# Wo as two groups of seven block products in the second to fourth pair of chunks

## The chip, the cores and the metric

One core of a Trainium2 chip runs the whole program in one launch. The metric is the device time of that launch in microseconds (us); smaller is better. Five engines take part: PE (matrix products), DVE (VectorE), ACT (ScalarE), POOL (GpSimd) and SP, which only issues transfers. Each works through its own list of instructions in order and is held by semaphore waits written into that list.

## The reference

`x` is (8, 512, 512) in float32: 8 chunks of 512 tokens by 512 features.

```python
xn = layernorm(x)
q, k, v = xn @ Wq.T + bq, xn @ Wk.T + bk, xn @ Wv.T + bv
kv = cumsum((elu(k) + 1) * v, axis=tokens)              # no matrix: a running sum per feature
s = ((elu(q) + 1) * kv * SCALE) @ Wo.T + bo             # "context" @ Wo
h = silu(fwht(xn * SU_ug) @ W_gate.T * ..) * (fwht(xn * SU_ug) @ W_up.T * ..)   # 2048 wide
g = silu(fwht(h * SU_dp) @ W_down.T * ..)
out = x + s * g
```

Wq, Wk, Wv and Wo are 512 by 512, gate and up 512 to 2048, down 2048 to 512. `fwht` is folded into the weights once.

## The kernel before

**Precision and products.** Every float32 operand is held as two float16 parts, HI and LO, and each product of blocks takes three matmuls per 128 rows of contraction: HI by HI, HI by LO, LO by HI. Each matmul is 128 by 128 by 512.

**Pairs, groups and seven products.** The 8 chunks go in four pairs. In pair 0 the weights are prepared, and products are plain (`plain_tile`). In pairs 1 to 3 a *group* `g` treats two 128-row blocks of a weight (rows `fp` and `fp + 2`) against the two chunks of the pair and both halves of the contraction, as a 2 by 2 product of blocks by the Strassen-Winograd scheme: seven products P1 to P7 of 6 matmuls each (`product`, L1639) in place of eight. That takes sums of weight blocks (S1 to S4, made in `s_sums` L1216, `s_high` L760, `s_low` L1232) and of token blocks (T1 to T4, `x_sums` L1074, `t_low` L1090, `t_high` L705). There are 22 groups (`GROUPS`): 6 for K, V, Q, then gate and up in turn, gate at even `g`, up at odd `g`, `g` from 6 to 21.

**A group on PE** (`group`, L1655) is P4 of `g-1`, P6, P3 of `g-1`, P2, P7, P1 of `g+1`, P5. P1, P6, P7 and P4 go into one "chain" bank, copied out between them by ACT (`copy_sum`, L798, line L803); P2 and P5/P3 go into two other banks, and DVE adds them (`add`, L1102, line L1107). The four result tiles of a group are called C11, C22, C21, C12, in this order of work; C21 is read from the chain bank itself. P1 of `g+1` uses the chain bank of `g-1` and waits until C21 of `g-1` has been taken from it (`wait_bank`, L1616). P7 of `g` waits for ACT's copy of P6 (`copied`).

**A group on DVE** (`group`, L1440), in order: for `g-1` use C22, `hidden_low` C11, use C21, `hidden_low` C22, add C12; add C11 of `g`; for `g-1` use C12, `hidden_low` C21; add C22 of `g`, which waits for P5 of `g`, the group's last product; `hidden_low` C12 of `g-1`; use C11 of `g`. Then, in pair 1 alone, `s_low` of one late weight piece and `s_sums` of the next; then, in pairs 1 and 2, statistics of the next pair at `g` 16 and 18. "Use" of an up tile is `hidden` (L1146), of a gate tile nothing: so for even `g` DVE handles the up tiles of `g-1` in it.

**A group on ACT** (`group`, L874): copies after P6, P7 and P1, between them silu of gate tiles (L826) or the float16 part of up tiles (`hidden_high`, L833), and in pair 1 `s_high` (L770) after the copy of P1 of `g+1`.

**Late weight pieces.** The sums S1 to S4 of pieces 0 to 11 are made in pair 0; pieces 12 to 21 are made in groups 5 to 14 of pair 1 (`late_sums`). POOL loads each raw piece (512 KB, `load_blocks`, L627, issue L641) as soon as `s_sums` of the one before is done, and stores the sums (L646).

**Down and Wo.** Behind the groups PE runs, per chunk, four quarters of down (`down_part`, L1736: 192 matmuls per chunk) and then Wo as a plain product (`out_product`, L1766: 4 tiles of 12 matmuls, L1788). Before them DVE takes the context's maximum (`ctx_absmax` L1170), a scale from it (`ctx_scale`, L1177), and splits its eight tiles in HI and LO (`split_ctx`, L1181). ACT takes down through silu into `gates` (`silu_outs`, L893) and Wo into `s_f`/`gate_g` (`take_out`, L902), and DVE multiplies and adds x (`gated`, L1388). SP loads 1 MB per weight piece into a ring of five slots (`load`, L480), 32 loads a pair.

Of the kernel before, what the change touches and what calls it, by code (L numbers as in the profile page):

```python
# [30 lines left out]
LOADS = GROUPS + 2 * (KB + 1)  # L31
# [14 lines left out]
IS_GATE, IS_UP = 3, 4  # L46
# [34 lines left out]
R_BANK = (3, 4, 5, 6)  # L81
QUADS = (0, 2, 1, 3)
# [15 lines left out]

STATS_AT = (16, 18)

# [23 lines left out]
def kind_of(g):  # L124
    return g % 3 if g < QKV_GROUPS else IS_GATE + (g - QKV_GROUPS) % 2
# [10 lines left out]
def nth(p, g):  # L136

    return GROUPS * (p - 1) + g


def group_order(g):
# [4 lines left out]
    if g < GROUPS - 1:  # L146
        return head + [(g + 1, P1), (g, P5)]
    return head + [(g, P5), (g, P4), (g, P3)]


ORDER = [at for g in range(GROUPS) for at in group_order(g)]


# [11 lines left out]
def late_sums(g):  # L165

    n = S_RING + g - S_LATE_FROM
    return n if S_RING <= n < GROUPS else None
# [12 lines left out]
def build(nc, x, x_t, wk_t, wv_t, wq_t, wo_t, ug_t, down_t, vecs, ident_in, hada_in, signs_in, out):  # L181
    scr_g = nc.dram_tensor("scr_g", (GROUPS, P, 4096), F16, kind="Internal").ap()
# [3 lines left out]
    scr_o = nc.dram_tensor("scr_o", (P, 4096), F16, kind="Internal").ap()  # L186

    with ExitStack() as ctx_stack:
# [43 lines left out]

        def stage(q):

            return (s_f if q % 4 < 2 else gate_g)[:, q % 2, :]
# [42 lines left out]
        s_loaded, s_stored = sem("s_loaded"), sem("s_stored")  # L278
# [19 lines left out]
        o_hi, o_made = sem("o_hi"), sem("o_made")  # L298
        var_ready, rstd_ready, xn_ready, xp_done = sem("var_ready"), sem("rstd_ready"), sem("xn_ready"), sem("xp_done")
# [8 lines left out]
        quad_done, o_done = sem("quad_done"), sem("o_done")  # L308
# [38 lines left out]
        def o_weight(slot):  # L347
            return ring[:, slot, :].rearrange("p (k s n) -> p k s n", k=KB, s=2)
# [24 lines left out]

        def tokens(c):
# [5 lines left out]

        def tile(g, j):

            return work[:, 4 * (g % 3) + j, :]
# [16 lines left out]
        def wait_taken(eng, p, g, j):  # L400
# [4 lines left out]
            elif kind == V:  # L405
                eng.wait_ge(kv_made, 8 * p + 4 * (g // 3) + j + 1)
            else:
                eng.wait_ge(h_made, 32 * p + 4 * ((g - QKV_GROUPS) // 2) + j + 1)

        def wait_free(eng, p, g, j):  # L410

            if g < 3:
                eng.wait_ge(x_ready, 2 * p + 2)
                return
# [23 lines left out]
        def _(sp):  # L438
# [31 lines left out]
            def wait_used(p, n):  # L470

                cc, q = divmod(n - GROUPS, KB + 1)
                if n < GROUPS:
                    sp.wait_ge(product_done, products_to(p, n, P3))
                elif q < KB:
                    sp.wait_ge(quad_done, KB * (2 * p + cc) + q + 1)
                else:
                    sp.wait_ge(o_done, TB * (2 * p + cc + 1))

            def load(p, n):  # L480
                slot, q = slot_of(p, n), (n - GROUPS) % (KB + 1)
# [12 lines left out]
                if p == 1 and S_RING <= n < GROUPS:  # L494
                    sp.wait_ge(s_late_stored[n % 2], 16 * ((n - S_RING) // 2 + 1))
                if n < GROUPS:
                    src = scr_g[n, :, :]
                elif q < KB:
# [1358 lines left out]
```

## Time and profile before

| what | value |
|---|---|
| median of 3 runs | 1317.81 us (1315.25 to 1320.3) |
| the profiled execution, its own time | 1316.55 us |
| its span, first to last instruction | 1314.7 us |
| PE busy | 1282.7 us, 98% of the span |
| DVE busy | 845.1 us, 64% |
| ACT busy | 565.9 us, 43% |
| granted PE clock | 0.998 |

The profiled execution is 1.26 us under the median, and its time is 1.85 us over its span. Busy time is the length of an engine's instructions; "idle before" is the time in which an engine stood before an instruction, with what released it. Names such as L1788 are lines of the kernel before.

### The profile page before, as it was taken

What the parts mean: (1) busy time and instruction counts of PE and PEld (TensorE: products, weight loads), DVE (VectorE), ACT (ScalarE), POOL (GpSimd) and SP (SyncE); (2) the same over time, 40 slices, a digit from 0 to 9 for tenths busy, and PEclk for the clock granted to TensorE, in tenths of its full rate; (3) what the DMA queues carried; (4) which work ended last, traced back from release to release, by engine and by line L of the source; (5) the groups of instructions that cost most, each with busy time, mean ns of one, the idle gap of its engine ahead of it and who ended that gap; (6) DMA issues with size and microseconds to landing.
All of it is one profiled execution on the core that took longest, in us unless ns stands there. A gap on an engine that the chain in (4) does not pass through costs nothing.

```text
span 1314.7 us, 15854 instructions
## 1 busy us (share of the span) xinstructions
PE 1282.7 (98%) x6004; PEld 581.8 (44%) x6004; DVE 845.1 (64%) x1303; ACT 565.9 (43%) x851; POOL 63.3 (5%) x108
## 2 busy tenths in 40 slices
PE   5989999999999999999999999999999999999998
PEld 3534444444444444444444444444444444444443
DVE  6989999977756777766614755566542774455411
ACT  4875566530335655541304554442124554443011
POOL 1000111111000011100000000010000000000000
PEclk9999999999999999999999999999999999999999
DMA  9512453568765366634535332334455333323230
GB/s 371 211 64 88 168 191 114 205 233 301 200 251 187 112 232 224 225 127 148 205 123 200 119 114 111 128 133 156 160 167 164 119 109 116 128 99 126 98 126 32
DMA packets 54363, 209.91 MB, mean 160 GB/s; under 512 B 12048, under 2 KB 12304, under 8 KB 37648
## 3 DMA queue, kind: packets, MB, share of 16 engines
q1 hardware_dynamic: 45744, 179.55, 38.5%
q0 software_dynamic: 8544, 29.37, 6.6%
q8 instruction: 47, 0.77, 0.2%
q14 instruction: 28, 0.23, 0.1%
HBM read 163.78 MB, written 45.11 MB: 159 GB/s over the span
## 4 chain that ended last, share of the span: by engine, by line
PE 58%; DVE 3%; ACT 2%; issue 2%; DMA 1%; DVEq 0%; ACTq 0%
PE bank L1650 34%; PE bank L1756 19%; PE bank L1788 5%; DMA h_all<-scr_f 1%; ACT work L813 1%; DVE work L1123 1%; ACT work L816 1%; DVE work L1107 0%; DVE work L1113 0%; DVE work L1146 0%; ACT work L803 0%; ACT L813 0%; DVE h_all L1240 0%; ACT h_all L770 0%; DVE h_all L1155 0%
## 5 line engine op out<-in xcount | busy, mean ns | idle before, releaser
L1650 PE MATMUL bank<-xops,ring 128*128 128x512 f16 x2772 | 602.6, 379 | 5.4 <-DVE work L1107 2.8
L1650 PEld LDWEIGHTS bank<-xops,ring 128*128 128x128 f16 x2772 | 269.5, 98 | 337.6 <-issue 7.7
L1756 PE MATMUL bank<-h_all,ring 128*128 128x512 f16 x1536 | 333.3, 379 | 1.3 <-DMA ring<-scr_d 1.3
L1107 DVE TENSOR_TENSOR work<-bank,work 128x512 f32<-128x512 f32 x198 | 133.6, 685 | 164.5 <-PE bank L1650 152.1
L1553 PE MATMUL bank<-xops,ring 128*128 128x512 f16 x1008 | 228.2, 381 | 4.3 <-DVE ring L1212 4.3
L1756 PEld LDWEIGHTS bank<-h_all,ring 128*128 128x128 f16 x1536 | 150.2, 98 | 182.8 <-DMA ring<-scr_d 1.8
L803 ACT ACTIVATE work<-bank 128x512 f32<-128x512 f32 x198 | 117.8, 595 | 234.8 <-PE bank L1650 234.1
L1553 PEld LDWEIGHTS bank<-xops,ring 128*128 128x128 f16 x1008 | 98.3, 98 | 128.6 <-issue 10.2
L899 ACT ACTIVATE gates<-bank,d_out 128x512 f32<-128x512 f32 x32 | 19.3, 687 | 207.2 <-PE bank L1756 207.2
L1391 DVE TENSOR_TENSOR gates<-gates,s_f 128x512 f32<-128x512 f32 x16 | 11.1, 691 | 150.7 <-ACT s_f L914 150.7
L833 ACT ACTIVATE h_all<-work 128x512 f16<-128x512 f32 x128 | 77.9, 624 | 66.1 <-DVE work L1146 65.9
L1155 DVE TENSOR_TENSOR h_all<-work,h_all 128x512 f16<-128x512 f32 x128 | 87.4, 685 | 5.9 <-ACT h_all L833 4.7
L1788 PE MATMUL bank<-ctx,ring 128*128 128x512 f16 x384 | 84.2, 379 | 0.0
L1113 DVE SCALAR_TENSOR_TENSOR work<-work 128x512 f32<-128x512 f32 x64 | 44.1, 689 | 50.5 <-ACT work L816 50.2
L1788 PEld LDWEIGHTS bank<-ctx,ring 128*128 128x128 f16 x384 | 37.6, 98 | 45.3
L826 ACT ACTIVATE work<-bank,gate_out 128x512 f32<-128x512 f32 x56 | 38.2, 683 | 42.0 <-PE bank L1553 40.8
L826 ACT ACTIVATE work<-work,gate_out 128x512 f32<-128x512 f32 x72 | 51.1, 714 | 5.4 <-DVE work L1107 5.1
L1146 DVE SCALAR_TENSOR_TENSOR work<-work,up_out 128x512 f32<-128x512 f32 x72 | 52.1, 743 | 0.7 <-DVE mean_root L1052 0.4
L1146 DVE SCALAR_TENSOR_TENSOR work<-bank,up_out,work 128x512 f32<-128x512 f32 x56 | 41.8, 746 | 16.1 <-PE bank L1650 11.4
L1128 DVE TENSOR_TENSOR_SCAN work<-work 128x512 f32<-128x512 f32 x32 | 39.2, 1224 | 1.1
L813 ACT ACTIVATE work<-work,vec,i_attn 128x512 f32<-128x512 f32 x36 | 29.1, 807 | 9.5 <-DVE work L1107 9.5
L816 ACT ACTIVATE work<-work,vec,i_attn 128x512 f32<-128x512 f32 x36 | 28.8, 799 | 0.0
(178 smaller groups left out, 870.6 us busy)
## 6 DMA issues: line engine op xcount, KB each, us to landing
ring<-scr_g SPq DMA_DIRECT2D x66, 1024.0 KB, 4.9
ring<-scr_d SPq DMA_DIRECT2D x32, 1024.0 KB, 5.4
scr_g<-ring SPq DMA_DIRECT2D x22, 512.0 KB, 3.3
h_all<-in_ug_t SPq DMA_DIRECT2D x8, 1024.0 KB, 12.6
x_res<-in_x_t SPq DMA_DIRECT2D x32, 256.0 KB, 4.1
out<-x_res SPq DMA_DIRECT2D x32, 256.0 KB, 6.8
scr_g<-ring POOLq DMA_DIRECT2D x12, 512.0 KB, 4.4
work<-in_x_t SPq DMA_DIRECT2D x6, 1024.0 KB, 7.1
```

The lines of the kernel that those rows point to most:

```text
L803: act.activation(tile(g, j), chain_bank(g)[:, :], ACT.Copy).then_inc(copied, 1)
L813: act.activation(exp_tile(n), src, ACT.Exp, bias=vec[:, b + f:b + f + 1], scale=i_attn[:, m:m + 1])
L826: act.activation(tile(g, j), src, ACT.Silu, scale=gate_out[:, at:at + 1]).then_inc(act_tiles, 1)
L833: act.activation(h[:, i, TILE_OF[j], HI, :], tile(g, j), ACT.Copy).then_inc(h_hi, 1)
L1107: dve.tensor_tensor(tile(g, j), at[:, :], tile(g, j), ALU.add).then_inc(summed, 1)
L1113: dve.scalar_tensor_tensor(tile(g, j), exp_tile(n), 1.0, tile(g, j), ALU.min, ALU.add) \
L1146: dve.scalar_tensor_tensor(tile(g, j), src, up_out[:, at:at + 1], tile(g - 1, j), ALU.mult, ALU.mult).then_inc(h_made, 1)
L1155: dve.tensor_tensor(at[:, LO, :], tile(g, j), at[:, HI, :], ALU.subtract).then_inc(h_ready, 1)
L1553: mm = pe.matmul(plain_bank(g, j)[:, :], at[:, s, 2 * dh + kk, r, :], xops[:, kk, xs, PLAIN_B[dh][c], :], start=(n == 0), stop=(n == len(t ...
L1650: mm = pe.matmul(to[:, :], weight_of(slot, s, b, kk), xops[:, kk, xs, c, :], start=(a == 0 and m in (P1, P2, P5)), stop=(a == 5), skip_gro ...
L1756: mm = pe.matmul(bank[D_BANK[t]][:, :], w[:, t, ws, :], at[:, s, :], start=(a == 0 and b == 0 and n == 0), stop=(a == KB - 1 and b == KB - ...
L1788: mm = pe.matmul(bank[R_BANK[t]][:, :], o_weight(slot)[:, f, ws, cols], at[:, s, :], start=(n == 0), stop=(n == 3 * KB - 1))
```

## The change

In pairs 1 to 3 Wo becomes groups 22 and 23, kind `IS_O`, of seven products each. `out_product` stays for pair 0. Pair 0's arrays of Wo are laid out like a weight piece (`o_piece`) and stored to `scr_g`, and the late sums grow by two pieces (22 and 23), made in groups 15 and 16 of pair 1.

The context takes the part of the tokens: its blocks T1 to T4 are formed, and its maximum, scale, split and sums are spread over the groups. All of it stands in DVE's list at the end of a group, behind the use of C11 and ahead of the late sums (`context_ready`), and in ACT's list at the end of a group (`ctx_high`).

The late raw pieces 13 to 23 are no longer loaded by POOL but by ACT, behind `s_high` (`load_late`); piece 12 is still loaded by POOL. Wo's raw pieces take four transfers each.

Down uses other banks in these pairs, its last quarter goes tile by tile, so that silu can follow each tile, and the outputs read Wo's tiles and down's silu from other buffers.

```diff
-LOADS = GROUPS + 2 * (KB + 1)
+PIECES = GROUPS + 2
+LOADS = PIECES + 2 * KB
...
+CTX_MAX_AT = {7: range(0, 4), 8: range(4, 6), 9: range(6, 8)}
+CTX_SCALE_AT, CTX_SUMS_AT = 11, (11, 17)
+CTX_SPLIT_AT = {12: (0,), 13: (2, 3), 18: (4,), 19: (6, 7)}
+CTX_HIGH_AT = {12: ((0, 0), (0, 1)), 17: ((1, 0),), 19: ((1, 1),)}
+CTX_LOW_AT = {14: ((0, 0),), 15: ((0, 1),), 20: ((1, 0), (1, 1))}
...
     n = S_RING + g - S_LATE_FROM
-    return n if S_RING <= n < GROUPS else None
+    return n if S_RING <= n < PIECES else None
...
             # gpsimd
-            for n in range(GROUPS):
-                if n + 1 < GROUPS and n + 1 != S_RING:
+            for n in range(PIECES):
+                if n + 1 < S_RING:
                     load_blocks(n + 1)
                 store_sums(n)
...
+                if n == S_CTX:
+                    ctx_max_of(1)
+                elif n == S_STATS:
+                    load_stats(2, 0)
...
             # scalar
+            def load_late(n):
+
+                act.wait_ge(s_summed, n)
+                if n < GROUPS:
+                    for q in (2 * (n - QKV_GROUPS), 2 * (n - QKV_GROUPS) + 1):
+                        act.wait_ge(stage_stored[q % 4], 16 * (q // 4 + 1))
+                    act.dma_start(s_raw(n).rearrange("p k r n -> p (k r n)"), scr_f[n - QKV_GROUPS, :, :]) \
+                        .then_inc(s_late_loaded, 16)
+                else:
+                    for k in range(KB):
+                        act.dma_start(s_raw(n)[:, k, :, :], attn_rows(wo_t, n - GROUPS)[:, k, :, :]) \
+                            .then_inc(s_late_loaded, 16)
...
+            def ctx_high(p, kk, half):
+
+                act.wait_ge(ct_made, 2 * p + kk - 1)
...
+                    if half:
+                        act.wait_ge(ctx_split, 8 + 6 * p)
+                for b in (T1 + 2 * half, T2 + 2 * half):
+                    last = act.activation(ctx_block(kk, HI, b), gates[:, b - T1, :], ACT.Copy, scale=s_c[:, 0:1])
+                last.then_inc(ct_hi, 1)
...
             # scalar, group(p, g)
                 if p == 1 and late_sums(g - 1) is not None:
                     s_high(late_sums(g - 1))
+                    if late_sums(g) is not None:
+                        load_late(late_sums(g))
                 if g:
                     take(p, g - 1, C12)
                 take(p, g, C11)
+                for kk, half in CTX_HIGH_AT.get(g, ()):
+                    ctx_high(p, kk, half)
...
             # vector
+            def ctx_sums(p, kk):
+
+                b11, b12, b21, b22 = (ctx_f(4 * kk + n) for n in range(KB))
...
+                prep.after(dve.tensor_tensor(gates[:, 0, :], b12, b11, ALU.subtract))
+                dve.tensor_tensor(gates[:, 2, :], b22, b12, ALU.subtract)
+                prep.after(dve.tensor_tensor(gates[:, 1, :], b22, gates[:, 0, :], ALU.subtract))
+                dve.tensor_tensor(gates[:, 3, :], b21, gates[:, 1, :], ALU.subtract).then_inc(ct_made, 1)
...
             # vector, group(p, g)
                 use(p, g, C11)
+                context_ready(p, g)
                 if p == 1 and late_sums(g - 1) is not None:
                     s_low(late_sums(g - 1))
                 if p == 1 and late_sums(g) is not None:
                     s_sums(late_sums(g))
...
                 last_sums(p)
-                ctx_absmax(p)
-                ctx_scale(p)
-                for n in range(8):
-                    split_ctx(p, n)
                 if p < PAIRS - 1:
                     normalise_pair(p + 1)
-                out_scale()
...
             # tensor
+                    at = ctx_block(kk, xs, c) if g >= GROUPS else xops[:, kk, xs, c, :]
...
-                for t in range(TB):
+                for t in range(0 if p else TB):
                     out_product(2 * p, t)
```

## Rows read from the trace of the kernel before

**Rows 1.** The page: busy time of the engines, and the chain by line.
```profile
PE 1282.7 (98%) x6004; PEld 581.8 (44%) x6004; DVE 845.1 (64%) x1303; ACT 565.9 (43%) x851; POOL 63.3 (5%) x108
...
PE bank L1650 34%; PE bank L1756 19%; PE bank L1788 5%; DMA h_all<-scr_f 1%; ACT work L813 1%; DVE work L1123 1%; ACT work L816 1%; DVE work L1107 0%; DVE work L1113 0%; DVE work L1146 0%; ACT work L803 0%; ACT L813 0%; DVE h_all L1240 0%; ACT h_all L770 0%; DVE h_all L1155 0%
```
**Rows 2.** Chain of waits in time order: pair 3 (start us, us, what).
```profile
1071.48 132.26 PE bank L1650 x612
1203.74 5.18 PE bank L1756 x24
1208.92 2.59 PE bank L1650 x12
1211.51 36.26 PE bank L1756 x168
1247.77 10.36 PE bank L1788 x48
...
1299.57 10.38 PE bank L1788 x48
1309.97 0.79 ACT gate_g L914
```
**Rows 3.** Timeline of pair 3, group 10 (start us, us, engine, line).
```profile
1114.43 0.69 DVE L1107 TENSOR_TENSOR work<-bank,work 128x512 f32<-128x512 f32 x1 [3.19 <-PE bank L1650]
1115.04 1.41 DVE L1146 SCALAR_TENSOR_TENSOR work<-work,up_out 128x512 f32<-128x512 f32 x2
...
1117.02 0.60 ACT L803 ACTIVATE work<-bank 128x512 f32<-128x512 f32 x1 [0.57 <-PE bank L1650]
1117.08 0.75 DVE L1146 SCALAR_TENSOR_TENSOR work<-bank,up_out,work 128x512 f32<-128x512 f32 x1
1117.51 1.14 ACT L833 ACTIVATE h_all<-work 128x512 f16<-128x512 f32 x2
...
1120.90 0.60 ACT L803 ACTIVATE work<-bank 128x512 f32<-128x512 f32 x1 [2.25 <-PE bank L1650]
1122.20 0.60 ACT L803 ACTIVATE work<-bank 128x512 f32<-128x512 f32 x1 [0.70 <-PE bank L1650]
```
**Rows 4.** Timeline of pair 1: groups 9 and 10.
```profile
484.22 1.05 ACT L770 ACTIVATE h_all<-h_all 128x1024 f16<-128x1024 f32 x1
486.29 1.22 DVE L1240 TENSOR_TENSOR h_all<-h_all 128x1024 f16<-128x1024 f32 x1
487.67 0.42 DVE L1227 TENSOR_TENSOR h_all<-h_all 128x256 f32<-128x256 f32 x1 [0.17 <-DMA h_all<-scr_f]
...
490.53 0.74 DVE L1146 SCALAR_TENSOR_TENSOR work<-bank,up_out,work 128x512 f32<-128x512 f32 x1
...
491.39 0.77 PEld L1650 LDWEIGHTS bank<-xops,ring 128*128 128x128 f16 x5 [0.42 <-issue]
```
**Rows 5.** PE's timeline: stalls ahead of P1 in groups 8 and 14; start of pair 2.
```profile
473.17 54.73 PE L1650 MATMUL bank<-xops,ring 128*128 128x512 f16 x252 [0.27 <-DVE work L1146]
528.37 64.91 PE L1650 MATMUL bank<-xops,ring 128*128 128x512 f16 x300 [0.47 <-DVE work L1146]
...
699.30 13.11 PE L1650 MATMUL bank<-xops,ring 128*128 128x512 f16 x60
```
**Rows 6.** DVE's timeline behind the groups of pair 1.
```profile
604.55 4.23 DVE L999 TENSOR_REDUCE ctx_max<-ctx 128x1 f32<-128x512 f32 x7
608.82 0.16 DVE L1175 TENSOR_REDUCE ctx_max<-ctx_max 128x1 f32<-128x8 f32 x1
609.53 0.15 DVE L975 TENSOR_SCALAR pw<-ctx_max_all 128x1 f32<-128x1 f32 x1 [0.55 <-POOL ctx_max_all L620]
...
610.28 0.49 DVE L1185 TENSOR_SCALAR ctx<-ctx,s_c 128x512 f16<-128x512 f32 x1
...
611.59 0.49 DVE L1185 TENSOR_SCALAR ctx<-ctx,s_c 128x512 f16<-128x512 f32 x1
...
634.93 0.21 DVE L1386 TENSOR_SCALAR o_out<-i_c,o_in 128x1 f32<-128x1 f32 x1
```
**Rows 7.** DVE's timeline: the token sums of the next pair.
```profile
649.85 0.68 DVE L1081 TENSOR_TENSOR work<-work 128x512 f32<-128x512 f32 x1
...
652.51 1.22 DVE L1086 TENSOR_TENSOR xops<-work,xops 128x1024 f16<-128x1024 f32 x1
...
661.82 2.36 DVE L1096 TENSOR_TENSOR xops<-work,xops 128x1024 f16<-128x1024 f32 x2 [0.31 <-ACT xops L707]
```
**Rows 8.** Transfers issued between 430 and 600 us, median to landing.
```profile
ring<-scr_g SPq DMA_DIRECT2D x14, 1024.0 KB, 6.2
scr_g<-h_all POOLq DMA_DIRECT2D x10, 512.0 KB, 3.7
h_all<-scr_f POOLq DMA_DIRECT2D x9, 512.0 KB, 6.5
```
**Rows 9.** Line L641: least, median and most of its landings.
```profile
DMA to landing us min/median/max: 3.4/6.5/13.9
```

## What the change should do to the time

> **What bounds the kernel now.** I read the page first: PE is busy 98% of the span and the chain that ended last is almost all PE work [rows 1]. A kernel like that gains only by fewer matmuls, and loses whatever makes PE stand. Then I read the chain in order of time [rows 2]: a pair is one unbroken run of group products (612 matmuls in 132.26 us, 0.216 us each), down, Wo (48 matmuls in 10.36 us, again 0.216), down, Wo. Neither DVE nor ACT appears in the later groups. So the question is how far DVE and ACT are from appearing there. That is not told by 64% and 43%; it is told by the two hand-overs on which PE depends in each group, and I read those in the timelines.
>
> First hand-over: in an even group, P1 of the next group waits for DVE's use of C21. Let T be the moment at which the odd group's last product ends; the add at 1114.43 waits for it, so T is 1114.3 [rows 3]. DVE then runs add C22, C11 and C22 of the up group, a `hidden_low`, and C21, which ends at 1117.08 + 0.75 = 1117.83, T + 3.5. P1 ends where its copy begins, at 1122.20, and takes 6 x 0.216 = 1.3, so it starts at about 1120.8, T + 6.5. **In pairs 2 and 3 this hand-over has 2.95 us to spare.** In pair 1 the late sums sit in exactly this gap: `s_low` at 486.29, `s_sums` at 487.67, C21 ending at 490.53 + 0.74 = 491.27, and PE's next weight load at 491.39 [rows 4]. **In pair 1 nothing is to spare** (0.15 us: `s_sums` stood 0.17 for its data). T is here 491.4 - 6.5 = 484.9. The trace shows what happens when the hand-over is late: 0.27 and 0.47 us of stall in groups 8 and 14, released by DVE's L1146 [rows 5].
>
> Second hand-over: P7 waits for ACT's copy of P6. That copy ends at 1117.62; P7 ends where its own copy begins, 1120.90, and so starts at 1119.6 [rows 3]. Spare: 1.9 us.
>
> **The change, part by part.**
>
> *Fewer matmuls.* Wo takes 96 matmuls a pair now, and 2 x 7 x 6 = 84 after. 12 x 3 pairs = 36 matmuls x 0.216 = **-7.8 us** [rows 2]. The order of down's last quarter does not change its count, and the tail (one ACT step, 0.79 before, then a multiply and an add, then the store) keeps its length, as silu takes the place of the read of Wo: nothing.
>
> *Context work in odd groups, pair 1.* It stands behind the use of C11 and so starts at T + 1.45, ahead of the late sums and of C22 and C21 of the up group. There is no slack, so all of it goes to PE. Prices: seven maxima in 4.23, 0.60 each, the last reduction 0.2 with its wait; the scale 609.53 to 610.28, 0.75; a split 610.28 to 611.59, 1.3; the output scale 0.21 [rows 6]; four sums of blocks 649.85 to 652.51, 2.66 [rows 7]; a LO of a sum like L1146, 0.70 each [rows 3].
> - group 7: 4 maxima, 2.45
> - group 9: 2 maxima and the reduction, 1.45
> - group 11: scale, output scale, sums, 0.75 + 0.21 + 2.66 = 3.6
> - group 13: two splits, 2.6
> - group 15: two LO, 1.4
>
> Sum 11.5; less 5 x 0.15 of slack and less the 0.74 that stalls already: **+10.0 us**. The same kind of work in even groups (8, 12, 14, 18, 20) costs nothing: behind it DVE has only two adds to do in a gate group, and waits until T + 9 for P5 (the first of [rows 3] shows 3.19 us of such waiting).
>
> *The raw pieces on ACT's queue.* Before, POOL issued a load right behind `s_sums`. Now ACT issues it behind `s_high`, which ends at 485.27, T + 0.45 [rows 4]; add 0.3 for issue. It can't be seen in this trace how long a load from ACT's queue takes. Bounds: 3.4, the least that such a load took [rows 9], and 6.5, its median [rows 8]. Those median loads ran beside SP's 1 MB load, which is issued behind P3, 3.9 us into a group; the new place has the queue nearly to itself until then. I take 4.0, nearer the lower end for that reason. It then lands at T + 4.6, and DVE's own list reaches `s_sums` at T + 2.7 plus the context work: only group 9 (T + 4.15) and group 15 (four transfers, another 0.9 of issue, T + 5.5 against 4.1) wait for it: 0.4 + 1.4 = **+1.8 us**. With 3.4 this is +0.8, and with 6.5 each of five groups waits until T + 7.25, which is a rival below. The store of the sums (3.7 [rows 8]) moves later by the same stalls and has three groups to spare before SP reads it. From its page "DMA: Bandwidth & Descriptors", section "Anatomy of one DMA", the Trainium skill has a fit of 2.0 us plus the bytes over 436 GB/s, 3.2 us for 512 KB; all loads in this trace took longer, and by that figure this term would be near +0.7.
>
> *ACT's new waits, all three pairs.* In group 17 ACT waits at the group's end for the sums that DVE forms after T + 1.45: they end at T + 4.1, two HI copies take 1.14 as L833 does, and only then comes the copy of P6, 0.60: it ends at T + 6.0, where P7 could have begun at T + 5.3 less the handing over: 0.8. Queued behind that wait are all of ACT's copies. In group 19 ACT waits for the two last splits (T + 4.05) and by the same steps delays P7 by 0.85. In group 12 four HI copies (2.3) precede one silu and the copy: in pairs 2 and 3 they fit; in pair 1, behind `s_high` and the issue, I count 0.3, and 0.15 for the issue in group 6, where ACT is on the chain. Pair 1: 0.8 + 0.85 + 0.45 = **+2.1**; pairs 2 and 3: 1.65 each, **+3.3**.
>
> *Context work in odd groups, pairs 2 and 3.* Slack 2.95. Groups 7, 13, 17 and 19 (2.45 to 2.7) just fit; group 11 (3.6) does not, 0.65 each: **+1.3**.
>
> *Down stage.* DVE loses maxima, scale and splits, 604.55 to about 620.7 [rows 6], and PE's stage shrinks by 20.7 us a pair; the next pair's tokens are ready at 661.82 + 2.36 = 664.2 [rows 7] and PE needs them at 699.3 [rows 5], 35 us later, of which 15 stay: nothing on the path either way. SP's loads stay 32 of 1 MB a pair. The two new groups' own steps (Identity with bias for a copy, +0.2 each) fall in groups in which DVE and ACT have no gate or up work left: nothing.
>
> **Sum**: -7.8 + 10.0 + 1.8 + 2.1 + 3.3 + 1.3 = **+10.7 us**. On the profiled execution, 1316.55, that gives 1327.2; that execution is 1.26 under the median, so the median should be about 1328.5. I say **1328**.
>
> About 0.5% (6.6 us) is what a measurement of this kernel can tell from no change; so "slower" is above 1324.4, "faster" below 1311.2.
>
> **The rivals.**
> 1. *Slow loads.* The load from ACT takes 6.5 us as POOL's did. Then `s_sums` starts at T + 0.75 + 6.5 = T + 7.25 against a limit of T + 2.85 in groups 7, 9, 11, 13 and 15: 4.4 x 5, and 0.9 more in the last, 22.9 in place of 10.0 + 0.74 + 1.8 = 12.5, so 10.4 more: 1339. For: it is the median of nine. Against: the place is free of SP's load, and the spread of 3.4 to 13.9 on one queue [rows 9] says that what lies beside a transfer decides. Chance 0.15.
> 2. *The cover holds* (the other side). DVE's order is not what limits P1: for example PE's wait for C21 is met from a later margin than I read, and ACT's waits are short. Then the -7.8 stands with at most 1 us of stall: 1310, faster. It decides where the sum of new stalls is below 1.2 us. Against: the 0.27 and 0.47 stalls have just this releaser [rows 5]; I find 18. Chance 0.07.
> 3. *Half of it.* Pair 1's DVE work costs as counted, but ACT's waits and group 11 in pairs 2 and 3 are absorbed, and loads land at T + 4: -7.8 + 10.0 + 0.8 + 0.5 = +3.5, 1321, within 0.5%. Chance 0.2.
> 4. My forecast, 1324.5 to 1332: 0.58.
>
> The Trainium skill says ("DMA: Bandwidth & Descriptors", "Issuing engines are not separate DMA queues") that issuing from another engine only saves issue time and brings no bandwidth. By that rule alone the loads would go on taking 6.5 us, which is rival 1; no row here shows a load from ACT's queue.
>
> **How the numbers follow.** The range takes rival 3 and rival 1: **1317 to 1339**; outside stay rival 2 and the ends, under 2 in 10. Faster 0.07, same 0.2, slower 0.73.
>
> **What would show each step.** In the changed trace: 24 x 42 = 1008 group matmuls a pair, and 96 plain Wo matmuls in all (pair 0). Stalls of PE in pair 1, released by DVE's use of C21, in groups 8, 10, 12, 14 and 16, of about 2.3, 1.7, 3.5, 2.5 and 2.6; 0.8 ahead of P7 in groups 18 and 20 of each pair, released by ACT's copy; pairs 2 and 3 each about 2.3 us of new idle time. PE's busy time down by 7.8. If the stalls before `s_sums` name the transfer rather than DVE's own work, rival 1 is right; if pair 1 shows no stalls at its even groups, my reading of the slack is wrong.

## The result, and the profile of the changed kernel

The changed kernel takes 1335.92 us (1335.83 to 1336.08, 3 runs) against 1317.81: ratio 1.0136, interval 1.0112 to 1.0159. It is slower, by 18.1 us; my sum said 10.7. The two profiled executions are 19.5 apart (1336.08 and 1316.55; spans 1334.3 and 1314.7). Of all the executions behind this text one, of experiment 1's even kernel, took 2777 us, and no ratio counts it.

The page of the changed kernel, busy time and the costliest group (columns of the group: line and form, busy us, mean ns, idle time before it):

```profile
PE 1280.4 (96%) x5968; PEld 578.5 (43%) x5968; DVE 882.6 (66%) x1368; ACT 586.3 (44%) x878; POOL 60.8 (5%) x101
...
L1822 PE MATMUL bank<-xops,ring 128*128 128x512 f16 x2772 | 608.3, 381 | 26.1 <-DVE work L1258 16.9
```

The 36 matmuls are gone (6004 to 5968 [rows 1]), but PE's busy time fell by 2.3 us and not by 7.8. L1822 is what L1650 was; L1258 is the use of C21, L1146 before. Its 16.9 us of stall were 0.7 before. PE's waits (total, times, longest):

```profile
PE bank L1822 <- DVE work L1258: 16.9, 7, 5.3
...
PE bank L1822 <- ACT work L891: 5.3, 9, 0.8
```

PE's timeline places them. The first five rows begin inside groups 8, 10, 12, 14 and 16 of pair 1, each with P1 of the next group; the next two begin with P7 of groups 18 and 20. The last three are the same places in groups 12, 18 and 20 of pair 2, and pair 3 repeats them.

```profile
476.76 18.29 PE L1822 MATMUL bank<-xops,ring 128*128 128x512 f16 x84 [2.40 <-DVE work L1258]
496.33 18.29 PE L1822 MATMUL bank<-xops,ring 128*128 128x512 f16 x84 [1.28 <-DVE work L1258]
519.91 20.31 PE L1822 MATMUL bank<-xops,ring 128*128 128x512 f16 x84 [5.29 <-DVE work L1258]
542.69 18.29 PE L1822 MATMUL bank<-xops,ring 128*128 128x512 f16 x84 [2.47 <-DVE work L1258]
565.38 18.48 PE L1822 MATMUL bank<-xops,ring 128*128 128x512 f16 x78 [4.40 <-DVE work L1258]
584.62 18.36 PE L1822 MATMUL bank<-xops,ring 128*128 128x512 f16 x84 [0.77 <-ACT work L891]
603.73 10.53 PE L1822 MATMUL bank<-xops,ring 128*128 128x512 f16 x48 [0.76 <-ACT work L891]
...
835.83 53.26 PE L1822 MATMUL bank<-xops,ring 128*128 128x512 f16 x246 [0.51 <-DVE work L1258]
889.85 18.30 PE L1822 MATMUL bank<-xops,ring 128*128 128x512 f16 x84 [0.77 <-ACT work L891]
908.91 10.53 PE L1822 MATMUL bank<-xops,ring 128*128 128x512 f16 x48 [0.76 <-ACT work L891]
```

Read the second column too: 84 matmuls take 18.29 us behind most stalls and 20.31 behind the one of 5.29. The windows of that trace (stretch, its length in us, busy of PE, PEld, DVE, ACT, POOL, then the granted clock, DMA share, GB/s) show why:

```profile
393.35:719.00 325.65, 306.10 (x1394) 135.85 (x1392) 213.30 (x333) 137.12 (x206) 12.94 (x22) 0.98 0.49 170
...
520.00:530.00 10.00, 10.00 (x38) 4.07 (x38) 7.89 (x14) 7.70 (x13) 0.54 (x1) 0.80 0.22 59
562.00:572.00 10.00, 6.62 (x24) 2.73 (x25) 7.99 (x15) 5.11 (x8) 0.00 (x0) 0.83 0.47 157
```

Behind the two long stalls the granted clock is 0.80 and 0.83 for 10 us: for a part of them it was at the level of 1.2 GHz. PE is fully busy in 520:530 and still runs 38 matmuls, where 10 us hold 46 at 0.216.

**Where the 19.5 us lie.** Pair 1, from its first group product to pair 2's, takes 325.65 us (393.35 to 719.00) against 307.42 (391.88 to 699.30 [rows 5]): +18.2. Pair 2 takes 305.18 and took 305.24. Pair 0 is 1.5 longer, mainly by one stall on DVE's L1362 (2.25 us where there were 0.56) that three other kernels with the same pair 0 (`e_early_max`, `e_even_schedule`, `e_stats_later`) have at 0.56 or 0.57 too; the kernel before by itself spreads over 5 us. So the loss is pair 1.

Two more causes stand ahead of the stalls in groups 12 and 16. Groups 9 to 11, DVE, ACT and POOL:

```profile
491.18 0.16 DVE L1288 TENSOR_REDUCE ctx_max<-ctx_max 128x1 f32<-128x8 f32 x1
...
497.99 0.33 ACTq L835 DMA_DIRECT2D h_all<-scr_f  x1
498.32 1.05 ACT L826 ACTIVATE h_all<-h_all 128x1024 f16<-128x1024 f32 x1
...
502.04 0.53 POOL L695 DMA_DIRECT2D scr_g<-h_all  x1 [8.74 <-DVE h_all L1394]
...
502.37 0.42 DVE L1381 TENSOR_TENSOR h_all<-h_all 128x256 f32<-128x256 f32 x1 [0.63 <-DMA h_all<-scr_f]
...
510.90 0.38 POOL L670 PARTITION_ALL_REDUCE ctx_max_all<-ctx_max  x1 [8.33 <-issue]
...
511.31 0.15 DVE L1081 TENSOR_SCALAR pw<-ctx_max_all 128x1 f32<-128x1 f32 x1 [1.77 <-POOL ctx_max_all L670]
```

The maxima are ready at 491.3; the all-reduce over them (one maximum out of those of all partitions) starts at 510.9, 8.9 us after POOL's store of a late sum, and DVE's scale stands 1.77 us for it. What POOL does in these 8.9 us is told in the last section. The ACT rows and L1381's show the new load in group 10. ACT's list has it behind `s_high`, and yet it is issued ahead of that conversion (497.99 and 498.32), sooner than the prediction had it. DVE waits 0.63 for it, the only wait for such a load in the pair, and in an even group, where it costs PE nothing. Group 15's end:

```profile
549.72 0.53 POOL L695 DMA_DIRECT2D scr_g<-h_all  x1 [10.05 <-DVE h_all L1394]
550.24 1.09 POOL L666 DMA_DIRECT2D s_f<-in_x  x2
551.32 1.07 POOL L666 DMA_DIRECT2D gate_g<-in_x  x2
...
553.34 0.42 ACTq L839 DMA_DIRECT2D h_all<-in_wo_t  x1
553.79 1.99 ACTq L839 DMA_DIRECT2D h_all<-in_wo_t  x3
...
561.63 0.42 DVE L1381 TENSOR_TENSOR h_all<-h_all 128x256 f32<-128x256 f32 x1 [3.28 <-DMA h_all<-in_wo_t]
```

POOL has just issued the next pair's rows for the statistics when ACT issues Wo's raw piece; DVE stands 3.28 us for it, where I had 1.4. The page's DMA issues of the changed kernel (KB each, median us to landing):

```profile
scr_g<-h_all POOLq DMA_DIRECT2D x12, 512.0 KB, 5.8
h_all<-scr_f ACTq DMA_DIRECT2D x9, 512.0 KB, 3.4
...
h_all<-in_wo_t ACTq DMA_DIRECT2D x8, 128.0 KB, 4.5
```

### The profile page after: what moved, and what is told of

Same layout as the page of the kernel before. It is cut to its first block, busy times and chain, and to the rows that moved or that the text cites. A ratio compares the mean times of both kernels' runs of the same rounds, so it can differ in the third digit from the quotient of the medians.

```text
span 1334.3 us, 16052 instructions
## 1 busy us (share of the span) xinstructions
PE 1280.4 (96%) x5968; PEld 578.5 (43%) x5968; DVE 882.6 (66%) x1368; ACT 586.3 (44%) x878; POOL 60.8 (5%) x101
## 4 chain that ended last, share of the span: by engine, by line
PE 53%; DVE 6%; issue 4%; ACT 2%; DMA 0%; ACTq 0%; DVEq 0%; POOL 0%; POOLq 0%
PE bank L1822 34%; PE bank L1941 19%; DVE work L1258 1%; ACT work L908 1%; DVE work L1233 1%; ACT work L911 1%; DVE work L1217 0%; DMA h_all<-in_wo_t 0%; DVE ctx L1302 0%; ACT work L891 0%; DVE h_all L1267 0%; DVE h_all L1394 0%; DVE gates L1312 0%; DVE gates L1313 0%; DVE gates L1311 0%
## 5 line engine op out<-in xcount | busy, mean ns | idle before, releaser
L1822 PE MATMUL bank<-xops,ring 128*128 128x512 f16 x2772 | 608.3, 381 | 26.1 <-DVE work L1258 16.9
L1822 PEld LDWEIGHTS bank<-xops,ring 128*128 128x128 f16 x2772 | 269.5, 98 | 363.5 <-issue 30.4
L1007 ACT ACTIVATE ctx<-bank,d_out 128x512 f32<-128x512 f32 x24 | 16.5, 687 | 193.6 <-PE bank L1941 193.6
L1258 DVE SCALAR_TENSOR_TENSOR work<-work,up_out 128x512 f32<-128x512 f32 x72 | 53.2, 743 | 0.5 <-DVE mean_root L1158 0.4
L1558 DVE TENSOR_TENSOR ctx<-ctx,s_f 128x512 f32<-128x512 f32 x6 | 4.1, 691 | 71.8 <-ACT ctx L1007 71.8
L1258 DVE SCALAR_TENSOR_TENSOR work<-bank,up_out,work 128x512 f32<-128x512 f32 x56 | 41.7, 745 | 6.2 <-issue 3.8
L1558 DVE TENSOR_TENSOR ctx<-ctx,gates 128x512 f32<-128x512 f32 x12 | 8.3, 693 | 53.8 <-ACT ctx L1007 53.8
L1822 PE MATMUL bank<-ctx,ring 128*128 128x512 f16 x144 | 34.5, 379 | 0.0
L908 ACT ACTIVATE work<-work,vec,i_attn 128x512 f32<-128x512 f32 x36 | 29.1, 807 | 9.5 <-DVE work L1217 9.5
L1167 DVE TENSOR_TENSOR work<-work 128x2048 f32<-128x2048 f32 x6 | 13.7, 2286 | 24.1 <-DMA work<-scr_m 24.1
```

The costliest lines, as they stand in the source:

```text
L908: act.activation(exp_tile(n), src, ACT.Exp, bias=vec[:, b + f:b + f + 1], scale=i_attn[:, m:m + 1])
L1258: dve.scalar_tensor_tensor(tile(g, j), src, up_out[:, at:at + 1], tile(g - 1, j), ALU.mult, ALU.mult).then_inc(h_made, 1)
L1822: mm = pe.matmul(to[:, :], weight_of(slot, s, b, kk), at, start=(a == 0 and m in (P1, P2, P5)), stop=(a == 5), skip_group_check=True)
```

## The experiments

Each kernel is set against the kernel before, run on the same chip, and ratios are to that one. Stalls are those of PE's timeline in pair 1, in the order of groups 8, 10, 12, 14, 16, 18, 20.

**1. Only DVE work, in odd or in even groups.** Both edits are to the kernel before: four maxima (2.45 us) behind the use of C11, with the late sums behind them. The maxima repeat work done again later.

```diff
                 use(p, g, C11)
+                if p == 1 and g in (7, 9, 11, 13, 15):     # e_even_work: (8, 10, 12, 14, 16)
+                    dve.wait_ge(ctx_made, 8 * p + 8)
+                    for n in range(4):
+                        last = absmax(ctx_max[:, n:n + 1], ctx_f(n))
+                    prep.after(last)
```

> The kernel before, with four more maxima of context tiles (2.4 us of DVE work, results unused) behind the use of C11 in groups 7, 9, 11, 13 and 15 of pair 1. Theory (an odd group of pair 1 has no slack on DVE ahead of P1): each 2.4 reaches PE less 0.15, so 5 x 2.3 less the 0.74 that stood already, +10.5 to +11.5 us, with stalls of PE of 2.3 to 2.4 us in groups 8, 10, 12, 14, 16. Rival (the stalls of the changed kernel come from the loads on ACT's queue or the maximum on POOL, and DVE has room): under +2 us.

> The same four maxima in groups 8, 10, 12, 14 and 16 of pair 1 in place of 7 to 15. Theory (only the place counts): 0 to +1 us. Rival (DVE is simply too full in pair 1, wherever the work stands): +8 us or more, as in the odd groups.

Odd: 1328.04 us, 1.0093 [1.0069, 1.0117]. Even: 1319.42, 1.0021 [1.0011, 1.0031]. PE's timeline of the odd one:

```profile
476.72 18.29 PE L1655 MATMUL bank<-xops,ring 128*128 128x512 f16 x84 [2.40 <-DVE work L1146]
497.42 18.29 PE L1655 MATMUL bank<-xops,ring 128*128 128x512 f16 x84 [2.40 <-DVE work L1146]
518.11 18.29 PE L1655 MATMUL bank<-xops,ring 128*128 128x512 f16 x84 [2.41 <-DVE work L1146]
538.81 18.29 PE L1655 MATMUL bank<-xops,ring 128*128 128x512 f16 x84 [2.40 <-DVE work L1146]
557.72 46.78 PE L1655 MATMUL bank<-xops,ring 128*128 128x512 f16 x216 [0.62 <-DVE work L1146]
```

2.45 us of work less 0.05 is each stall: the odd groups of pair 1 have no slack, and the theory of the prediction is shown in its plainest form. In group 16 only 0.62 come, because in the kernel before the last late sum stands in group 14. The new stalls are 9.5 us, and pair 1 of the profiled execution is 9.8 longer than before (317.23 against 307.42); of the 11.9 found, 1.4 lie in pair 0 of that execution, which the edit leaves alone. The same work in even groups costs 3.3 us in all, above the 0 to 1 that I had given; 1.9 of it lie in pair 1. Its stalls are 0.64, 0.88 and 0.91 where there were 0.27 and 0.47. DVE does no more ahead of C21 there, but it waits 0.84, 1.08 and 1.11 for the loads of groups 9, 11 and 13 (before: 0.17 in group 9): the loads hang on the sums of the even groups, which now come later. In the odd kernel the blocks of 84 stay at 18.29: no clock is lost behind stalls of 2.4.

**2. The change with its context work in even groups.** All of DVE's context work moves to even groups; ACT's HI copies stand in odd ones.

```diff
-S_CTX, S_STATS = 16, 20
+S_CTX, S_STATS = 14, 20
-CTX_MAX_AT = {7: range(0, 4), 8: range(4, 6), 9: range(6, 8)}
-CTX_SCALE_AT, CTX_SUMS_AT = 11, (11, 17)
-CTX_SPLIT_AT = {12: (0,), 13: (2, 3), 18: (4,), 19: (6, 7)}
-CTX_HIGH_AT = {12: ((0, 0), (0, 1)), 17: ((1, 0),), 19: ((1, 1),)}
-CTX_LOW_AT = {14: ((0, 0),), 15: ((0, 1),), 20: ((1, 0), (1, 1))}
+CTX_MAX_AT = {6: range(0, 4), 8: range(4, 8)}
+CTX_SCALE_AT, CTX_SUMS_AT = 10, (10, 16)
+CTX_SPLIT_AT = {12: (0, 2), 14: (3,), 18: (4, 6, 7)}
+CTX_HIGH_AT = {11: ((0, 0),), 13: ((0, 1),), 17: ((1, 0),), 19: ((1, 1),)}
+CTX_LOW_AT = {12: ((0, 0),), 14: ((0, 1),), 20: ((1, 0), (1, 1))}
```

> The changed kernel with all of DVE's context work moved to even groups (maxima 6 and 8, scale and first sums 10, splits 12, 14 and 18, second sums 16, LO parts 12, 14 and 20; ACT's HI parts in 11, 13, 17, 19). Theory: the stalls in groups 8, 10, 12, 14 of pair 1 and those of pairs 2 and 3 go, the 36 matmuls saved remain, and what is left is the wait for Wo's raw pieces in group 16: 7.8 saved, 1 to 4 given back: 1311 to 1315 us where before gives 1318. Rival (the loads on ACT's queue hold DVE in every odd group): stalls of 1 us or more stay in groups 8 to 16, 1320 or more.

1318.64 us, 1.0020 [1.0009, 1.0031]: above the band I gave. With the same work, the same queues and the same matmuls, all but 2.5 of the 18.1 us are gone. In the profiled execution pair 1 is still 6.5 us longer than before (313.96 against 307.42), and what follows it 5.1 shorter (610.27 against 615.40), which is what 24 fewer matmuls make. What is left stands in two rows, the first of DVE's timeline, the second of PE's:

```profile
549.67 0.42 DVE L1381 TENSOR_TENSOR h_all<-h_all 128x256 f32<-128x256 f32 x1 [4.42 <-DMA h_all<-in_wo_t]
...
553.42 47.37 PE L1822 MATMUL bank<-xops,ring 128*128 128x512 f16 x210 [4.22 <-DVE work L1258]
```

The other stalls are 0.69, 0.91, 1.01 and 0.83, behind waits of DVE for the late loads. The one of 4.22 is Wo's raw piece, and 210 matmuls take 47.37 where 0.216 each makes 45.4: about 1.9 us of clock. Groups 18 and 20 have no stall of over 0.2; pair 2 has none but the 0.2 and 0.3 of its first groups, which stand in every kernel here.

**3. The maximum earlier.** POOL's all-reduce is moved one piece ahead in POOL's list, ahead of the store behind which it was late.

```diff
-S_CTX, S_STATS = 16, 20
+S_CTX, S_STATS = 15, 20
```

> The changed kernel with pair 1's maximum over the partitions placed on POOL one store earlier (behind the store of piece 15 in place of 16). Theory (the 1.77 us that DVE waited for POOL in group 11 made the stall so long that the granted clock fell): group 12's stall goes from 5.3 to about 3.5, the clock's 2 us go with it if the shorter stall keeps it at full: -2 to -4 us against the changed kernel, 1332 to 1334. Rival (the clock falls at 3.5 too, or POOL is as late again): -2 or 0.

1334.24 us, 1.0131 [1.0114, 1.0147]: no difference from the change's 1.0136 that can be measured. The rows are POOL's all-reduce and PE's groups 8, 12 and 14:

```profile
475.14 19.94 PE L1822 MATMUL bank<-xops,ring 128*128 128x512 f16 x84 [2.40 <-DVE work L1258]
...
502.26 0.58 POOL L670 PARTITION_ALL_REDUCE ctx_max_all<-ctx_max  x1 [8.92 <-issue]
...
518.09 18.29 PE L1822 MATMUL bank<-xops,ring 128*128 128x512 f16 x84 [3.44 <-DVE work L1258]
538.86 19.98 PE L1822 MATMUL bank<-xops,ring 128*128 128x512 f16 x84 [2.47 <-DVE work L1258]
```

DVE's wait for POOL is gone and group 12's stall is 3.44, against 5.29 and my 3.5. So 1.8 of that stall was POOL's, and the rest of it the work as counted. But the clock now falls behind the stalls of 2.40 and 2.47, which had cost nothing in the change, 1.7 us each; DVE waits 4.08 for Wo's raw piece in place of 3.28, and group 16's stall is 5.21; and the all-reduce again stands 8.92 behind the store ahead of it.

**4. Wo's piece in one transfer; the late loads on POOL's queue; ACT's last copies one group later.** The first is an edit to experiment 2, the others to the change.

```diff
 # e_wo_one
-                    for k in range(KB):
-                        act.dma_start(s_raw(n)[:, k, :, :], attn_rows(wo_t, n - GROUPS)[:, k, :, :]) ...
+                    w = wo_t.rearrange("p k (r f n) -> p f (k r) n", r=2, f=2)[:, n - GROUPS, :, :]
+                    act.dma_start(s_raw(n).rearrange("p k r n -> p (k r) n"), w) ...
 # e_pool_loads
-                if n + 1 < S_RING:
+                if n + 1 < PIECES and n + 1 != S_RING:
                     load_blocks(n + 1)
...
-                    if late_sums(g) is not None:
-                        load_late(late_sums(g))
 # e_late_high
-CTX_HIGH_AT = {12: ((0, 0), (0, 1)), 17: ((1, 0),), 19: ((1, 1),)}
+CTX_HIGH_AT = {12: ((0, 0), (0, 1)), 18: ((1, 0),), 20: ((1, 1),)}
```

> The kernel of e_even_schedule with each raw piece of Wo loaded by one transfer in place of four. Theory (the four issues on ACT's queue, 2.2 us together, and their landing make the 4.42 us that DVE stood in group 15, and with it the 4.2 us stall of PE and the clock's 1.9 us): landing in 3.5 to 4.5 us from one issue, stall in group 16 down from 4.2 to about 1, -4 to -5 us against e_even_schedule, 1313 to 1315. Rival (short rows of 512 B from the weight are what is slow, however issued): stall 3 us or more, no more than -1.5 us.

> The changed kernel with the late raw pieces loaded by POOL as before (Wo's by four transfers). Theory (the context work in odd groups is the main cost; the queue costs only in group 15): stalls of 2.4, 1.3, 3.5 or more and 2.5 stay in groups 8, 10, 12 and 14, group 16's goes from 4.4 to about 1.5, in all -3 to -5 us, 1331 to 1333. Rival (the change of queue is the main cost): back to 1320 or less.

> The changed kernel with ACT's HI parts of the second half of the context in groups 18 and 20 in place of 17 and 19. Theory (ACT stands at the end of 17 and 19 for DVE's sums and splits, ahead of the copy of P6): the stalls of 0.77 and 0.76 in groups 18 and 20 go in all three pairs, 6 x 0.76 = -4.6 us, 1331; DVE's own 0.2 or less may show in their place. Rival (ACT's copy would be late by its own work anyway): -1 us or less.

*One transfer:* 1319.25 us, 1.0020 [1.0008, 1.0032]; DVE waits 5.10 for it and the stall is 4.90. Four issues were not what made it late; this theory falls. The first was issued at 544.9, as POOL's loads for the statistics (542.97 to 545.1) were under way, and took 8.8 us; the second, without them, took 4.4.

*POOL's queue:* 1337.79 us, 1.0159 [1.0133, 1.0185]; I had expected a gain of 3 to 5. Its rows show group 11's late load held behind the all-reduce:

```profile
511.76 0.38 POOL L670 PARTITION_ALL_REDUCE ctx_max_all<-ctx_max  x1 [8.98 <-issue]
512.02 0.74 POOL L694 DMA_DIRECT2D h_all<-scr_f  x1
...
512.17 0.15 DVE L1083 TENSOR_SCALAR pw<-ctx_max_all 128x1 f32<-128x1 f32 x1 [2.44 <-POOL ctx_max_all L670]
```

DVE waits 2.44 for POOL and then 1.41 for the load, and group 12's stall is 7.27. Groups 8, 10 and 14 stall by 2.40, 1.29 and 2.46, as in the change: the move to ACT's queue costs nothing there and helps in group 12. DVE waits 3.12 for Wo's piece here too, so it is not ACT's queue that makes that late.

*ACT's copies later:* 1333.69 us, 1.0122 [1.0104, 1.0140], 1.4 us under the change's 18.1, which these intervals can't tell from nothing; 4.6 were expected. The stalls of 0.77 and 0.76 are gone in all three pairs (0.83 by DVE in their stead in group 18 of pair 1), so the two steps on ACT were right and worth some 3.8 us: behind pair 1 this execution is 3.5 shorter than the change's. Four blocks of 84 in this execution take 19.98, 19.75, 19.98 and 19.98 us, 6.5 together over what 18.29 each would be, against 3.4 of such loss in the change. Pair 1 is 2.7 longer than the change's (328.34), 3.1 of it clock: what the edit took away, the clock took back in this execution.

**5. The statistics' load one step later, in the change.**

```diff
-S_CTX, S_STATS = 16, 20
+S_CTX, S_STATS = 16, 21
```

> The changed kernel with POOL's first load of the next pair's statistics tokens (1 MB in four transfers) behind the store of piece 21 in place of 20. Theory (in group 15 Wo's raw piece lands late because this load was issued just ahead of it, not because of four transfers or short rows): DVE's wait of 3.28 us there goes to under 1, PE's stall in group 16 from 4.4 to 1.5 to 2, -2.5 us and up to 1.5 more of clock: 1332 to 1334. Rival (the transfer from the weight is slow by itself): no change.

1335.65 us, 1.0143 [1.0128, 1.0157]: no gain. PE's groups 16 and 18, and DVE's two waits for Wo's pieces:

```profile
559.21 0.43 DVE L1381 TENSOR_TENSOR h_all<-h_all 128x256 f32<-128x256 f32 x1 [0.79 <-DMA h_all<-in_wo_t]
...
562.97 17.10 PE L1822 MATMUL bank<-xops,ring 128*128 128x512 f16 x78 [1.92 <-DVE work L1258]
...
571.39 0.43 DVE L1381 TENSOR_TENSOR h_all<-h_all 128x256 f32<-128x256 f32 x1 [2.25 <-DMA h_all<-in_wo_t]
...
582.46 18.36 PE L1822 MATMUL bank<-xops,ring 128*128 128x512 f16 x84 [2.40 <-ACT work L891]
```

Taken away from the first piece, the load now lies beside the second. The first piece's wait falls from 3.28 to 0.79 and its stall from 4.40 to 1.92, which shows that the bulk load beside it made most of Wo's delay (2.5 of 3.28). The 78 matmuls take 17.10, not 18.48, which gives the clock's price in the change's group 16: 1.4 us. The second piece's wait gives 1.6 of it back in group 18 (0.77 to 2.40), and the clock more: blocks of 84 at 19.98 and 20.03 in groups 8 and 12, 3.4 over, where the change had 2.0. The profiled execution is 2.0 us shorter than the change's, but 1.8 of it is pair 0; pair 1 (325.31) gains 0.3, as the median does.

**6. A schedule that keeps the gain.** Three edits on top of experiment 4's first kernel: in `e_sums_first` the late sums go ahead of the context's work in DVE's list and the load of odd groups ahead of `s_high`; `e_first_stats` has the statistics' load one step later; `e_load_sooner` has the load of odd groups ahead of the copy of P7.

```diff
 # e_sums_first, scalar and vector
+                if p == 1 and g % 2 and late_sums(g - 1) is not None and late_sums(g) is not None:
+                    load_late(late_sums(g))             # behind the copy of P7
...
-                    if late_sums(g) is not None:
+                    if g % 2 == 0 and late_sums(g) is not None:
                         load_late(late_sums(g))         # behind s_high, as before
...
                 use(p, g, C11)
-                context_ready(p, g)
                 ...
                     s_sums(late_sums(g))
+                context_ready(p, g)
 # e_first_stats
-S_CTX, S_STATS = 14, 20
+S_CTX, S_STATS = 14, 21
 # e_load_sooner
-                copy_sum(p, g, 2)
                 if p == 1 and g % 2 and late_sums(g - 1) is not None and late_sums(g) is not None:
                     load_late(late_sums(g))
+                copy_sum(p, g, 2)
```

> The kernel of e_wo_one with the late sums ahead of the context work in DVE's list, and for odd groups ACT's load issued behind the copy of P7 in place of behind the next group's. Theory (in e_even_schedule the stalls of 0.7 to 1.0 in groups 8 to 14 are DVE waiting for a load issued too late): they shrink to 0.3 or less, -2 to -3 us against e_wo_one, 1310 to 1312, which is the saving of 36 matmuls with nothing given back. Rival (the stalls are DVE's own list): no change.

> The kernel of e_sums_first with the same move of the statistics load. Theory: the stall of 3.64 us in group 16 falls to 1 or less and the half clock behind it goes: -3.5 to -4.5 us against e_sums_first, 1311 to 1312 where before gives 1316 to 1317: faster than before by 0.3 to 0.4%. Rival (as above): no change, 1315.5.

> The kernel of e_first_stats with ACT's load in odd groups issued ahead of the copy of P7, 1.2 us sooner. Theory (what is left of the stalls in groups 8 to 14, 1.06, 0, 0.96 and 0.72, is the landing of this load): -1.5 to -2.5 us more, 1309 to 1310. Rival (ACT then stands for DVE's sums ahead of the copy and makes P4 late): +1 us or more.

1315.53 us, 0.9983 [0.9967, 1.0000]; 1313.16, 0.9967 [0.9954, 0.9980]; 1313.76, 0.9983 [0.9973, 0.9992]. All three are above what was expected of them. In the first, stalls of 1.06, 0.96 and 0.72 stay where 0.3 was expected, and group 16 has 3.64. The statistics' load one step later takes that to 1.41 and its slow clock away, though DVE still waits 1.61 for Wo's first piece, which takes 6.7 us with no such load beside it and took 8.9 with it. The second is the best kernel of this study: ahead of the kernel before by 3.6 us (its six runs lie from 1311.21 to 1314.09), and of the change by over 20. That it is faster than before is shown; by 0.5%, no. The gain lies behind pair 1 (5.1 us); pair 1 itself is still 2.2 longer than before (309.63). PE's timeline of it has no stall over 1.41 in these groups and no slow block:

```profile
510.60 18.29 PE L1821 MATMUL bank<-xops,ring 128*128 128x512 f16 x84 [0.77 <-DVE work L1259]
530.13 18.29 PE L1821 MATMUL bank<-xops,ring 128*128 128x512 f16 x84 [1.25 <-DVE work L1259]
549.83 14.40 PE L1821 MATMUL bank<-xops,ring 128*128 128x512 f16 x66 [1.41 <-DVE work L1259]
565.51 2.76 PE L1821 MATMUL bank<-xops,ring 128*128 128x512 f16 x12 [1.28 <-DVE work L1218]
```

The third kernel takes the stalls of groups 12 and 14 down to 0.26 and 0.31, and then Wo's second piece meets the statistics' load: DVE waits 3.34 for it and PE 3.07, by L1218, ahead of a P3. I had expected 1.5 to 2.5 less; nothing was gained.

**7. One long stall.** In the kernel before, eight maxima (4.85 us) in group 11 alone, to see the clock without the rest.

```diff
                 use(p, g, C11)
+                if p == 1 and g == 11:
+                    dve.wait_ge(ctx_made, 8 * p + 8)
+                    for n in range(8):
+                        last = absmax(ctx_max[:, n:n + 1], ctx_f(n))
+                    prep.after(last)
```

> The kernel before with eight more maxima (4.85 us) behind the use of C11 in group 11 of pair 1 alone. Theory (one stall of PE of 4.7 us makes the granted clock fall for a while behind it, as behind the 5.29 of the changed kernel, at a price of 2 us): 4.7 + 2 = +6 to +7 us, and the 84 matmuls behind the stall take 20.3 us in place of 18.3. Rival (the clock's fall has another cause): +4.7 and 18.3.

1324.28 us, 1.0052 [1.0036, 1.0067]: +7.5 for 4.85 us of work. PE's row behind the stall, and the window around it:

```profile
515.37 85.71 PE L1655 MATMUL bank<-xops,ring 128*128 128x512 f16 x384 [4.78 <-DVE work L1146]
```
```profile
515.00:522.00 7.00, 6.63 (x19) 2.49 (x20) 4.60 (x9) 4.37 (x7) 0.00 (x0) 0.60 0.20 69
```

384 matmuls at 0.216 and the 0.15 that each such row has beyond that make 83.1; the row has 85.71, 2.6 more, at a granted clock of 0.60 in the first microseconds. With no context work of the change, no new queue and no Wo in the groups, one stall of 4.78 costs 7.4. Pair 1 of this execution is 8.0 longer; most of the rest is group 8's stall, 1.14 where there were 0.27, ahead of the edit's place, less group 14's 0.47, which is gone. The forecast was 6 to 7 us in all.

## Why the prediction was right, and where not

1328 was forecast, 1317 to 1339 as the range, 0.73 for slower. The sign and the mechanism hold; 18.1 came where the sum had 10.7. 1335.9 lies above the 1324.5 to 1332 that had the chance of 0.58, and inside the range only because its upper end was taken from a rival that the trace refutes: in that the range was lucky.

**Matmuls, -7.8: right.** 36 fewer are on the page, and pair 2, where -2.6 met 2.0 of new stalls and the 0.15 of three new rows, came out at -0.06 against my -0.3. That busy time fell by only 2.3 is the slow clock (3.4 more) and the 0.15 that every row behind a new stall has over 0.216 a matmul, a dozen of them.

**Context work in odd groups, pair 1: right.** Stalls of 2.3, 1.7, 3.5, 2.5 and 2.6 were forecast and 2.40, 1.28, 5.29, 2.47 and 4.40 came. Experiment 1 shows the rule by itself, experiment 2 that even groups are nearly free. Group 10's is 0.4 under: the prediction had ACT issue group 9's load 0.75 us after the odd group's last product, and it was issued 1 us before it (487.48), so DVE did not wait. Of the two that are over, each by 1.8, neither is DVE's work:

- *The scale's place in group 11.* I priced it as work alone (0.75) and did not ask when its input is there. POOL's list in the change has the all-reduce between the stores of the late sums, and I put no time on that list: it came 8.9 us after a store, 1.77 too late, and 8.1 of that time lie behind POOL's reconfiguration (last section). Experiment 3 gives the 1.8 back in that stall.
- *Wo's raw piece.* I took 4.0 us for each load and added issue time. For the `scr_f` loads that was too high (3.4, and a wait of 0.63); for Wo's it was too low. The prediction says itself that "what lies beside a transfer decides", and then looks only at SP's load; the statistics' load, which POOL issues 1 to 3 us ahead of it, is the neighbour that decided: without it the wait is 0.79, under the 1.4 of the sum (experiment 5).

**The clock, nothing in the sum, 3.4 us measured** (2.0 in group 12, 1.4 in group 16). This is a term that was left out. The longest stall in pair 1 of before is 1.26 us (459.78, in its first groups), with its 60 matmuls at full speed behind it, so that trace has no row for it. Experiment 7 isolates it: 2.6 us behind 4.78.

**ACT's waits, right in all three pairs:** 0.77 and 0.76 for 0.8 and 0.85, three times, and gone in `e_late_high`. The 0.45 counted for groups 12 and 6 of pair 1 did not come. **Group 11's overrun in pairs 2 and 3:** 0.51 for 0.65. **The down stage and the places in even groups, nothing:** right.

The terms together for pair 1: stalls are 17.4 and were 0.74, so 16.6 more; the clock 3.4; fewer matmuls -2.6; 17.4 of the 18.2 found. The remaining 0.8 is the 0.15 by which each stall costs more than its length, as a row behind a stall is that much longer: pair 1 has five such rows more. 1.5 of the profiled execution's 19.5 are pair 0's.

**The rivals.** *Slow loads* gave 1339, near the result, and is false as a mechanism: the loads landed in 3.4, not 6.5, and DVE waited 0.63 for one of nine. A number that is met for another reason confirms nothing. The Trainium skill's rule behind it ("DMA: Bandwidth & Descriptors", "Issuing engines are not separate DMA queues") could not be tried cleanly: in `e_pool_loads` these loads land in 6.4 from POOL against 3.4 from ACT, but they also start at another time, beside other traffic. The same page's fit of 2.0 us plus bytes over 436 GB/s ("Anatomy of one DMA"), which it gives for transfers that GpSimd issues, makes an estimate of 3.2 us for 512 KB; these nine, which ACT issued, landed in 3.2 at the least and 3.4 in the median. *The cover holds* and *half of it* fall with the first row of PE's stalls.

## What to carry to other kernels

Before placing work on an engine that is 64% busy, read for each place the time between that engine's hand-over and the moment the bound engine asks for it: the same five times 2.45 us made 9.5 us of new stalls in odd groups and 1.7 in even ones, and the whole change went from +18.1 to +2.5 us by renumbering its places. For each moved step ask also when its input will be there, whether its engine must be reconfigured just ahead of it, and what bulk load will be on the engines beside a transfer that something waits for. A stall of several microseconds can cost half as much again in clock, so one long wait is worse than its length, and a saving elsewhere may be eaten by it.

## What was not expected of the hardware

**The clock behind stalls is not a function of their length alone.** Blocks of 84 matmuls behind stalls of 2.40 to 2.47 took 18.29 eight times (all four in `e_odd_work`, both in the change, one each in `e_pool_loads` and `e_stats_later`) and 19.93 to 19.98 six times (both in `e_early_max` and `e_late_high`, the other one in those two); behind 3.44 one took 18.29, behind 4.34 to 7.27 five took 19.75 to 20.43. A stall of 3.07 in `e_load_sooner` cost 1.7. So the price is 0 or 1.5 to 2.6 us (the last in experiment 7), and which of them is not foreseen from these rows.

**POOL's all-reduce stood behind its own reconfiguration, not behind the store.** In pair 1 of the change it starts 8.33 us after the store's issue has ended, and in the nine other kernels built on the change 6.42 to 8.98, each time with no releaser in the timeline ("issue") and with its input ready. The view of the all-reduce's line in 500 to 512 us and the transfers that POOL issued at 502 show what lies between:

```profile
L670 POOLq MODIFY_POOL_CONFIG  x2: 37/37/37, 502.8 to 502.8; - x2
...
scr_g<-h_all POOLq DMA_DIRECT2D x1, 512.0 KB, 4.0
```

The store had landed 4.0 us after its issue, 4.9 us before the all-reduce started, and in all ten traces it had landed 1.7 us or more ahead of it. Right behind the store's issue stand, in all ten, two instructions MODIFY_POOL_CONFIG that the kernel's text does not have, 6.2 to 8.8 us ahead of the all-reduce. Where they stand far ahead the delay does not show: in pair 2 of the change they are at 724.3, and the all-reduce starts at 813.62, 0.14 us after its maximum; in the kernel before they are at 573.9 and the all-reduce at 609.12, 0.14 behind its maximum too. They appear where POOL changes from the root of the variances (`rstd`) to the all-reduce or back; in `e_pool_loads` `rstd` starts 8.7 us behind its own (590.4 and 599.10), 1.4 us after its input and with no releaser. The Trainium skill ("GPSIMD Engine Reference", "Instruction dispatch") says that the first call of freshly loaded POOL code costs some 6 us, counted from this instruction, that no instruction in the profile shows; here it is 6.2 to 8.8 us, and the measurement decides. All this is read from traces: no run moved the reconfiguration alone.

**One transfer in place of four did not land sooner** beside a bulk load (8.8 us for the whole 512 KB), though ACT spent 0.55 to 0.65 us on issuing it against some 2 for the four.
